# Where SP puts two loads of whole weight pieces among the fetches of split pieces, in a float32 feed-forward kernel on one Trainium2 core

## What is computed

```python
x = x + L0_ffn(L0_cond(x, cond, ...))   # conv1d, 9 taps, 4 groups, + context; then y = u @ W.T + b + LoRA
x = x + L1_ffn(L1_cond(x, cond, ...))   # per-batch 64x64 mix; then a gated low-rank FFN:
    scores = xf @ Wr.T                  # 64 experts, the best 16 kept, softmax gates G
    h = einsum('nd,krd->nkr', xf, A)    # 1024 -> 64*16
    out = einsum('nkr,kdr->nd', h * G, B) * 2.0   # 64*16 -> 1024
```

## Time and profile before

| | us |
|---|---|
| median of 3 runs | 658.79 |
| lowest, highest | 657.31, 658.83 |
| the profiled execution, its own time | 658.74 |
| its span, first to last instruction | 656.9 |
| granted TensorE clock, mean | 0.999 of full |
| HBM traffic | 131.94 MB read, 25.71 MB written, 240 GB/s over the span |

### The profile page before, as it was taken

The page is one execution under the profiler, slowest core; times in us unless marked ns, Lnnn a source line. Parts: engine busy times, 40 slices in busy tenths (PEclk is TensorE's granted clock), DMA queues, the critical chain, the costliest instruction groups (busy, mean ns, idle before and its releaser), DMA issues.

```text
span 656.9 us, 8354 instructions
## 1 busy us (share of the span) xinstructions
PE 649.5 (99%) x3197; PEld 537.6 (82%) x3197; DVE 451.2 (69%) x690; ACT 213.3 (32%) x275; POOL 73.1 (11%) x91
## 2 busy tenths in 40 slices
PE   9999999999999999999999999999999999999997
PEld 8878888888897788888788788888879888888875
DVE  2859569549377798468769658637868857656765
ACT  2714134333144125335134212334313311334510
POOL 1499300000000250000000051000000000000000
PEclk9999999999999999999999999999999999999999
DMA  8577715975969826777975672374986764047585
GB/s 306 206 291 273 303 49 156 354 234 208 397 230 394 331 107 281 273 219 275 358 267 214 260 292 96 129 214 156 385 319 243 290 248 165 0 137 230 193 335 199
DMA packets 51594, 157.98 MB, mean 240 GB/s; under 512 B 5488, under 2 KB 6384, under 8 KB 51568
## 3 DMA queue, kind: packets, MB, share of 16 engines
q1 hardware_dynamic: 46240, 148.05, 61.7%
q10 hardware_dynamic: 5328, 9.61, 4.7%
HBM read 131.94 MB, written 25.71 MB: 240 GB/s over the span
## 4 chain that ended last, share of the span: by engine, by line
PE 89%; DMA 6%; DVE 3%; issue 1%; SPq 1%; ACT 0%; DVEq 0%; POOL 0%; POOLq 0%
PE bank L1374 23%; PE bank L1376 23%; PE bank L1375 23%; PE bank L1388 9%; DMA piece_lo<-kept 6%; PE bank L1408 3%; PE bank L1395 2%; PE bank L1414 1%; PE bank L1400 1%; PE bank L1402 1%; PE bank L1415 1%; PE bank L1370 1%; DVE x L925 1%; DVE u_lo L1012 1%; DVE work L932 1%
## 5 line engine op out<-in xcount | busy, mean ns | idle before, releaser
L893 DVE TENSOR_TENSOR piece_lo<-raw,piece_hi 128x1024 fp32r<-128x1024 f32 x60 | 74.2, 1240 | 93.2 <-ACT piece_hi L646 93.2
L646 ACT ACTIVATE piece_hi<-raw 128x1024 fp32r<-128x1024 f32 x60 | 63.3, 1057 | 148.0 <-PE bank L1376 102.7
L1374 PE MATMUL bank<-piece_hi,u_hi 128*128 128x512 f32 x272 | 107.9, 397 | 0.1
L1375 PE MATMUL bank<-piece_lo,u_hi 128*128 128x512 f32 x272 | 107.3, 395 | 0.0
L1376 PE MATMUL bank<-piece_hi,u_lo 128*128 128x512 f32 x272 | 107.3, 395 | 0.0
L1374 PE MATMUL bank<-v_hi,piece_hi 128*128 128x512 f32 x256 | 101.8, 398 | 0.0
L1376 PE MATMUL bank<-v_hi,piece_lo 128*128 128x512 f32 x256 | 101.1, 395 | 0.0
L1375 PE MATMUL bank<-v_lo,piece_hi 128*128 128x512 f32 x256 | 101.0, 394 | 0.0
L1374 PE MATMUL bank<-piece_hi,v_hi 128*128 128x512 f32 x192 | 76.3, 397 | 1.8 <-DMA piece_lo<-kept 1.4
L1376 PE MATMUL bank<-piece_hi,v_lo 128*128 128x512 f32 x192 | 75.8, 395 | 0.0
L1375 PE MATMUL bank<-piece_lo,v_hi 128*128 128x512 f32 x192 | 75.7, 394 | 0.0
(11 more groups left out here) (143 smaller groups left out, 799.4 us busy)
## 6 DMA issues: line engine op xcount, KB each, us to landing
raw<-pieces SPq DMA_DIRECT2D x76, 512.0 KB, 5.5
piece_hi<-kept SPq DMA_DIRECT2D x48, 512.0 KB, 5.3
piece_lo<-kept SPq DMA_DIRECT2D x48, 512.0 KB, 6.3
x<-x SPq DMA_DIRECT2D x16, 512.0 KB, 5.1
gate_x<-gates ACTq DMA_DIRECT2D x32, 256.0 KB
out<-x SPq DMA_DIRECT2D x32, 256.0 KB, 4.4
conv_in<-conv_x SPq DMA_DIRECT2D x15, 516.0 KB, 6.7
conv_in<-pieces SPq DMA_DIRECT2D x12, 512.0 KB, 8.5
```

Source lines behind the costliest of these rows:

```text
L646: act.activation(piece_hi[:, n % SLOTS, :], raw[:, r % RAWS, :], ACT.Copy).then_inc(s_piece_hi, 1)
L893: dve.tensor_tensor(piece_lo[:, n % SLOTS, :], raw[:, r % RAWS, :], piece_hi[:, n % SLOTS, :].bitcast(F32), ALU.subtract).then_inc(s_piece ...
L1374: pe.matmul(to, left_hi, right_hi, start=first, stop=False)
L1375: pe.matmul(to, left_hi, right_lo, start=False, stop=False)
```

## The change

In the out stage of groups 1 to 3, SP issues the loads of the raw pieces 32 and 33 later: behind the fetches of the kept pieces 28 and 29 instead of behind those of 26 and 27. All waits, buffers and the other engines' programs stay as they are.

```diff
                 next_raw(24)
                 next_raw(25)
-                fetch(g, 26)
+                for n in range(26, 29):
+                    fetch(g, n)
                 next_raw(32)
-                fetch(g, 27)
+                fetch(g, 29)
                 next_raw(33)
-                for n in range(28, 31):
-                    fetch(g, n)
+                fetch(g, 30)
                 for t in range(2):
                     store(g, t, 0, 3 + t)
                 fetch(g, 31)
```

## The result

The change makes the kernel slower: 662.31 us (median of 13 runs, 660.58 to 665.04) against 657.96 us for the kernel before in the same 13 rounds. The ratio is 1.0054, 95% interval [1.0039, 1.0068], so 3.5 us or 0.54%. The forecast was 659.6 us, no measurable change, with a range that ended at 661.3.

What follows compares the result with a forecast made beforehand. PE's stream of matmuls was taken to set the time, with waits at step 31. Terms 0 + 0 + 0 + 0.84 us on the 658.79 us median, or on the 658.74 us profiled execution, gave 659.6 us; range 657.6 to 661.3.

Steps and rivals of the forecast that it cites:

- Steps 32 and 33: Steps using the moved raw loads: loads land with 5 and 4 us to spare in group 1; cost 0.
- the fourth part: Step 31: the same 15 units stand ahead in either order; the queue may run dry after fetches 26 and 27.
- The 0.56 us for group 1's two gaps: DMA engines idle 0.28 us each after fetches 26 and 27 in group 1, not regained before step 31.
- the term for step 31: Later landing of step 31's piece in groups 1, 2 and 3: 0.56, 0.28 and 0, in all 0.84 us.
- The landing moves PE one to one: Any shift in step 31's landing shifts PE equally, since PE already waits for it.
- That of 30 within half a us of now: Profile sign: step 30's low half lands within half a us of its present time after issue.
- The low halves of 27 and 28: Profile sign: these land about 1.0 and 2.1 us sooner after their issue than now.
- restarts are dear: Rival, chance 0.12: fetches into an empty queue after 26 and 27 pay 1.4 us for some restarts; 661.6 us.
- never runs dry: Rival, chance 0.25: the DMA queue has no gap, step 31's landing stays to 0.1 us; time 658.8 us.
- the lightened queue moves faster: Rival, chance 0.12: pieces 28 and 29 arrive early, stalls vanish, step 31 comes in time; 657.1 us.
- my own case: Main case, chance 0.51: gaps in the queue delay step 31; reaches from 658.9 to 660.5 us.
- the bound upward: Upper limit of step 31's term: 0.56 us in each of three groups, 1.7 us.

Runs made afterwards that it cites:

- d_only_33: Against the kernel before, only raw load 33 moved, behind the fetch of 29; raw 32 stays behind fetch 26. Ratio 1.0001.
- c_one_later: Against the kernel before, both raw loads one fetch later, behind the fetches of 27 and 28. Ratio 1.0023.
- j_all_later: Against the kernel before, both raw loads behind fetch 30, still ahead of the stores and fetch 31. Ratio 1.0163.
- the filler: Two unused 0.131 MB HBM-to-HBM copies per group, added to the changed kernel behind fetches 26 and 27. Ratio 1.0043 to the kernel before.
- h_change_stores_behind: Against the kernel before, the change together with the two stores moved behind fetch 31. Ratio 0.9982.
- k_all_later_stores_behind: Against the kernel before, both raw loads behind fetch 30 and the two stores behind fetch 31. Ratio 1.0034.

## Why the prediction was wrong

**What held.** Step 31's kept piece is what PE waits for, and moving its landing moves the time: a unit fewer ahead of it gave 0.25%, and with it in time the change costs nothing that can be measured. The moved loads wait for nothing and cost SP nothing. Steps 32 and 33 had time: ACT's splits of 32 and 33 still waited for PE in all groups. The mechanism of the fourth part was right too: the same bytes stand ahead of step 31, and only a queue that runs short can hurt. The 0.56 us for group 1's two gaps is the 0.58 us found in its first two stretches. For zero, one and four gaps d_only_33, c_one_later and j_all_later have ratios of 1.0001, 1.0023 and 1.0163, so the queue does run short. By an estimate from the 358 GB/s of the Trainium skill (SBUF — State Buffer, section Summary: rules for kernel authors) a fetch would take 2.93 us and the queue would never run short. Where this and the trace differed, the trace was right.

**The step that failed** is the term for step 31, "0.56 + 0.28 + 0 = 0.84". It measured 2.5 us in the profile: the landing came 1.2, 0.3 and 1.0 us later in the groups. The timed runs say 3.5 us. The two profiled executions are not typical ones: that of the kernel before took 658.74 us, 0.8 above the median of the 13 runs, that of the changed kernel 660.71, 1.6 below its median. Where the rest of the 3.5 lies is not in them, and stays open. Two things were wrong in the term:

- It priced a gap as idle time at full rate and stopped there. By that price, 0.28 us per gap and group, one, two and four gaps cost 0.8, 1.7 and 3.4 us over three groups. They measured 1.5, 3.5 and, without the 3.1 of the clock, 7.6: about twice as much each time. In the profile, the first two stretches hold 1.0 us of the 2.5, close to the forecast's 0.84, and the three behind them another 0.8, in which a slow stretch of 309 to 358 GB/s comes in and the one of the kernel before goes. The last 0.7 is in none of the five.
- Group 3 got 0, because its fetch 26 landed late (5.9 us) and I took that as a property of the group. In the changed kernel it landed after 4.4 us, and in none of the other ten profiles after more than 4.7; the 5.9 was a matter of that execution. Its first two stretches were short in the kernel before as well, so the 0 fits them by luck; the 1.0 us came behind them.

"The landing moves PE one to one" held, but step 31 is not alone: steps 30 and 31 share the lateness, in group 1 0.55 and 0.92 us. "That of 30 within half a us of now" was wrong: 8.3 us against 6.7. The low halves of 27 and 28 were to land 1.0 and 2.1 us sooner; in group 1 it was 0.8 and 0.4, and that of 28 was already in the slow stretch.

**The rivals.** The one named "restarts are dear" is nearest to what happened: it gave 661.6 and slower, with a chance of 0.12, and needed 0.66 us per group; the runs show 1.2. Its price was 1.4 us for some of the restarts, seen as a late low half of a single fetch. What the runs show is a cost of about twice the idle time for each gap, so its form was another one. The rival "never runs dry" is excluded, and so is "the lightened queue moves faster". The range ended at 661.3, since my own case with a bound of 1.7 us held most of it; the bound upward assumed the full rate after a gap, the very thing that fails. The chance of 0.04 for over 0.3% faster rested on 1.7 us of waits in all; there were 2.6, but the change won none of them.

**What stays open**: why a gap costs twice its idle time, and why the rate sags. The trace gives the mean of 16 DMA engines, not each, so whether one of them falls behind was not seen. The sag is not tied to a moment of the stage, since it moves with the order: the fourth stretch from fetch 26 in the changed kernel, the sixth in the one before. In the kernel before it goes with the stores. In the changed kernel it follows the gaps: it is weaker after one gap, and all but gone with the filler in them. But there step 31 landed as late as without the filler, so how much of the lateness is the slow stretch's is not shown.

## What to carry to other kernels

Where SP feeds PE from one queue and PE paces the large fetches, keep some load in the queue behind the first of them: the order of loads that are early anyway decides when the last one lands. Ask first which transfer is waited for and what stands ahead of it, and move from there what nobody waits for (here the stores, 0.25%); a price for a gap that was only its idle time was too low by half here. If PE's wait gets long, look at its granted clock behind it, too: in j_all_later that was 3.1 of 10.7 us. A DMA share near 1 does not say that the engines could move no more: compare GB/s with the best stretch.

## What the runs showed of the hardware

- The DMA share reads 1.00 at 369 GB/s and 1.03 at 416: the share that a packet's time takes stays at 1 while a tenth of the rate is unused. The filler of 0.26 MB per group went in there without a measurable cost.
- There are stretches in which a filled queue moves less than that. After two gaps it was 309, 329 and 358 GB/s in the three groups of the changed kernel and 354 to 360 in h_change_stores_behind; after one gap (c_one_later) it was 372 to 383; with the filler in the gaps it was 414, 380 and 415. With stores in the queue and no gap it was 310, 307 and 345 in the kernel before, and 411, 410 and 404 at the same place with the stores moved.
- Stores cost the loads behind them more than their bytes: 0.524 MB to HBM delayed a landing by 1.9 to 2.7 us, where 1.26 us is its worth at 416 GB/s. Two copies of 0.131 MB from HBM to HBM cost 3.8 us over three groups, where 1.9 was expected.
- In j_all_later TensorE stood still for 3.5 us in group 1 and 2.2 us in group 3, and in k_all_later_stores_behind for 2.4 us in group 1. Each time the granted clock then went down to 0.50, the lower of its two levels, for about 3 us, which cost 1.5 us in each of the two groups of j_all_later. In group 2 of j_all_later, after 1.9 us, it stayed at 1.00.
